# Macaron block on one core: the output projection one round earlier, the turn of h2 moved forward

## The reference

```python
x = L0_attn_x                                      # (1, 1024, 256)
x = x + 0.5 * _L0_ffn_ref(_layernorm(x), ...)      # silu(gate) * up, weights rounded to fp8
x = x + _L0_attn_ref(_layernorm(x), ...)           # retention, below
x = x + 0.5 * _L0_ffn_ref(_layernorm(x), ...)      # the same weights again
...
q, k, v = split(x @ w_qkv);  q, k = _xpos(q), _xpos(k)           # 16 heads of 16
scores = einsum('bhtd,bhsd->bhts', q, k) * D ** -0.5 * mask      # causal, decaying
yn = group_norm(einsum('bhts,bhsd->bhtd', scores, v)) * gn_weight + gn_bias
return (silu(x @ w_g) * yn) @ w_proj
```

## Time and profile before

| what | value |
|---|---|
| time, median of 3 runs | 155.21 us (155.19 to 155.21) |
| the profiled execution's own time | 155.3 us, of which 153.5 us are its span |
| TensorE busy | 147.2 us, 96% of the span |
| VectorE, ScalarE, GpSimd busy | 121.4, 85.2 and 68.5 us |
| TensorE's granted clock | full speed in all slices of the span |

### The profile page before, as it was taken

How to read it: one execution, slowest core, us unless ns; L and a number is a source line. 1 busy time by engine, 2 the same in 40 slices (tenths; PEclk the granted TensorE clock), 3 DMA queues, 4 the chain that set the end, 5 groups by cost and what they waited for, 6 DMA issues and landing times.

```text
span 153.5 us, 3712 instructions
## 1 busy us (share of the span) xinstructions
PE 147.2 (96%) x1327; PEld 117.4 (76%) x1327; DVE 121.4 (79%) x271; ACT 85.2 (56%) x203; POOL 68.5 (45%) x76
## 2 busy tenths in 40 slices
PE   5999899999999999998999999999999999999992
PEld 2366588788989696967686969698877788888991
DVE  0797999999799485859688888899755999566784
ACT  2385998677232453547475656657676648453310
POOL 3447244775891700283845748573978220000000
PEclk9999999999999999999999999999999999999999
DMA  4999502903000000000000000000000000002114
GB/s 112 339 354 306 214 0 31 361 27 121 15 0 0 4 0 4 0 4 0 4 2 0 6 0 6 0 4 0 4 2 0 0 4 0 0 0 68 34 36 139
DMA packets 7009, 8.47 MB, mean 55 GB/s; under 512 B 448, under 2 KB 5712, under 8 KB 6992
## 3 DMA queue, kind: packets, MB, share of 16 engines
q1 hardware_dynamic: 6816, 8.16, 16.0%
q10 hardware_dynamic: 176, 0.07, 0.4%
HBM read 7.19 MB, written 1.05 MB: 54 GB/s over the span
## 4 chain that ended last, share of the span: by engine, by line
PE 74%; POOL 10%; DVE 6%; issue 4%; ACT 3%; DMA 2%; POOLq 0%; ACTq 0%; DVEq 0%
PE bank L1167 23%; PE bank L1195 14%; PE bank L1223 9%; POOL grstd L340 6%; PE bank L1280 5%; PE bank L1236 5%; PE bank L1250 4%; PE bank L1364 3%; PE bank L1309 3%; DMA xt<-in_L_attn_x 2%; POOL rstd L318 2%; PE bank L1262 2%; DVE stats L705 2%; PE bank L1296 1%; PE bank L1341 1%
## 5 line engine op out<-in xcount | busy, mean ns | idle before, releaser
L1167 PE MATMUL bank<-hh,up_r 128*128 128x512 f32 x92 | 25.5, 401 | 0.1
L1167 PE MATMUL bank<-hh,gate_r 128*128 128x512 f32 x92 | 25.6, 401 | 0.0
L1195 PE MATMUL bank<-down_r,fhi 128*128 128x256 f32 x96 | 24.3, 291 | 0.0
L340 POOL TENSOR_TENSOR grstd<-gve,neg_half 128x16 f32<-128x16 f32 x8 | 23.3, 2908 | 0.7
L1195 PE MATMUL bank<-down_r,flo 128*128 128x256 f32 x96 | 23.4, 281 | 0.0
L455 ACT ACTIVATE gact<-bank,vec 128x512 f32<-128x512 f32 x24 | 16.3, 684 | 9.0 <-PE bank L1167 8.1
L463 ACT ACTIVATE fhi<-fuse 128x512 fp32r<-128x512 f32 x24 | 14.6, 624 | 10.8 <-DVE fuse L752 10.8
L1167 PEld LDWEIGHTS bank<-hh,up_r 128*128 128x128 f32 x92 | 16.8, 188 | 4.3 <-issue 0.6
L1167 PEld LDWEIGHTS bank<-hh,gate_r 128*128 128x128 f32 x92 | 16.9, 188 | 4.0 <-ACT gate_r L404 0.4
L1195 PEld LDWEIGHTS bank<-down_r,fhi 128*128 128x128 f32 x96 | 18.1, 188 | 0.7 <-issue 0.2
L1195 PEld LDWEIGHTS bank<-down_r,flo 128*128 128x128 f32 x96 | 18.1, 188 | 0.6 <-issue 0.2
(11 more groups left out here) (90 smaller groups left out, 285.6 us busy)
## 6 DMA issues: line engine op xcount, KB each, us to landing
raw<-in_rotation SPq DMA_DIRECT2D x1, 1536.0 KB, 7.5
out<-xt SPq DMA_DIRECT2D x8, 128.0 KB, 1.8
raw<-in_L_ffn_down_w SPq DMA_DIRECT2D x2, 384.0 KB, 7.4
wqkv<-in_L_attn_w_qkv SPq DMA_DIRECT2D x1, 768.0 KB, 9.3
xt<-in_L_attn_x SPq DMA_DIRECT2D x2, 256.0 KB, 3.7
xt<-in_L_attn_x SPq DMA_DIRECT2D x1, 512.0 KB, 5.4
raw<-in_rotation SPq DMA_DIRECT2D x1, 512.0 KB, 3.5
raw<-in_L_ffn_gate_w SPq DMA_DIRECT2D x1, 384.0 KB, 6.2
```

The lines of the kernel that those rows point to most:

```text
L340: pool.tensor_tensor(grstd[:, c % 2], gve[:, :], neg_half[:, :], ALU.pow).then_inc(grstd_done, 1)
L1167: mm = pe.matmul(dst[:, :], wr[m][:, k * I + i * P:k * I + (i + 1) * P], half[:, k, g % NG, :], start=(k == 0 and half is hhi), stop=(k == ...
L1195: mm = pe.matmul(downs[d][:, 0:C], half[:, g % NG, i, t * P:(t + 1) * P], wr["down"][:, i * C:(i + 1) * C], start=(i == 0 and half is fhi) ...
```

## The change

`project_out` of tile c - 2 now stands in round c, behind `update_state(c)` and ahead of `values(c)`; before, round c held that of tile c - 3, behind `project_g`. `turn_h2(c + 2)` stands directly behind `project_v(c + 1)`, and ScalarE's `copy_h2(c + 2)` ahead of `copy_v(c + 1)`. VectorE's `add_proj(c - 2)` closes the round. Behind the loop `project_out(3)` falls away; VectorE's list for tiles 5, 6 and 7 is set anew, and GpSimd's `group_roots(5)` stands ahead of `add_state(6)`. Two waits in `turn_y` and `project_out` follow the new order.

```diff
--- before.py
+++ after.py
@@ -386,8 +386,8 @@
             add_state(5)
             roots(X_ROOTS + 8)
             roots(X_ROOTS + 9)
+            group_roots(5)
             add_state(6)
-            group_roots(5)
             group_roots(NT - 2)
             group_roots(NT - 1)
             roots(X_ROOTS + NT + 2)
@@ -610,9 +610,9 @@
             copy_y(1)
             for c in range(2, 6):
                 take_y(c - 1)
+                copy_h2(c + 2)
                 copy_v(c + 1)
                 gate_silu(c + 1)
-                copy_h2(c + 2)
                 affine(c - 2)
                 copy_qk(c + 1)
                 copy_y(c)
@@ -976,8 +976,6 @@
                 rotate(c + 1)
                 group_norm(c - 2)
                 mask_scores(c, 2)
-                if c >= 3:
-                    add_proj(c - 3)
                 mask_scores(c, 3)
                 group_var(c - 1)
                 norm_stats(NT + c + 3, NT + c + 4)
@@ -985,12 +983,12 @@
                 rotate_parts(c + 2)
                 mask_kv(c)
                 norm_tile(NT + c + 3)
+                add_proj(c - 2)
             mask_scores(5, 0)
             mask_scores(5, 1)
             rotate(6)
             group_norm(3)
             mask_scores(5, 2)
-            add_proj(2)
             mask_scores(5, 3)
             group_var(4)
             tile_stats(16)
@@ -998,26 +996,26 @@
             mean_var(16)
             gated(3)
             rotate_parts(7)
+            mask_kv(5)
             mean_var(17)
             tile_stats(18)
-            mask_kv(5)
             mean_var(18)
+            add_proj(3)
+            tile_stats(19)
+            mean_var(19)
             mask_scores(6, 0)
             mask_scores(6, 1)
             rotate(7)
             group_norm(4)
             mask_scores(6, 2)
+            mask_scores(6, 3)
             group_var(5)
-            add_proj(3)
-            mask_scores(6, 3)
-            tile_stats(19)
             norm_tile(16)
-            mean_var(19)
+            norm_tile(17)
             mask_kv(6)
-            norm_tile(17)
             norm_tile(18)
+            norm_tile(19)
             gated(4)
-            norm_tile(19)
 
             c, j0 = NT - 1, NG * NI
             mask_scores(c, 0)
@@ -1025,8 +1023,8 @@
             mask_scores(c, 2)
             mask_scores(c, 3)
             add_proj(c - 3)
+            group_var(c - 1)
             group_norm(c - 2)
-            group_var(c - 1)
             tile_stats(2 * NT + 4)
             mean_var(2 * NT + 4)
             gated(c - 2)
@@ -1335,8 +1333,7 @@
                     pe.wait_ge(gd_done, c)
                     if c >= 2:
                         pe.wait_ge(ga_done, c - 1)
-                    if c >= 3:
-                        pe.wait_ge(x2_done, c - 2)
+                        pe.wait_ge(x2_done, c - 1)
                 for k in range(KC):
                     mm = pe.transpose(b_turned_y[c][:, k * P:(k + 1) * P], yT[:, c % 2, k, :], ident)
                 mm.then_inc(y_turned, 1)
@@ -1358,7 +1355,7 @@
                 pe.wait_ge(go_done, c + 1)
                 if c == 0:
                     pe.wait_ge(wp_in, 16)
-                pe.wait_ge(gd_done, min(c + 3, NT - 2))
+                pe.wait_ge(gd_done, min(c + 2, NT - 2))
                 pe.wait_ge(ga_done, c + 1)
                 for k in range(KC):
                     mm = pe.matmul(b_gn[c][:, C:2 * C], go[:, k, :], wp[:, k, :], start=(k == 0), stop=(k == KC - 1))
@@ -1444,21 +1441,19 @@
             for c in range(2, 6):
                 turn_y(c - 1)
                 project_v(c + 1)
+                turn_h2(c + 2)
                 project_g(c + 1)
-                if c >= 3:
-                    project_out(c - 3)
-                turn_h2(c + 2)
                 turn_qk(c + 1)
                 turn_gn(c - 2)
                 project_qk(c + 2)
                 apply_state(c)
                 update_state(c)
+                project_out(c - 2)
                 values(c)
                 scores(c + 1)
             turn_y(5)
             project_v(7)
             project_g(7)
-            project_out(3)
             turn_qk(7)
             apply_state(6)
             update_state(6)
```

## The result

The changed kernel takes 156.55 us (156.37 to 156.96) against 155.19 (155.06 to 155.21): a ratio of 1.0093, with an interval of 1.0079 to 1.0107, 1.36 us slower. The forecast was 156.3, slower, in a range of 155.4 to 157.0. The profiled execution's span is 154.7 us instead of 153.5.

A forecast was written before the change was run, and what follows sets the result against it. TensorE, busy in nearly every slice, was taken to bound the kernel. Costs of +1.88 us in the loop and -0.11, -0.25 and -0.42 behind it gave +1.10, from 155.21 to 156.3, range 155.4 to 157.0.

The forecast's parts named there:

- The place of the projection: Projection between update_state and values, rounds 2 to 5: two changes of array shape cost 0.32 us per round.
- rival (B): Projection between the narrow steps costs nothing beyond its own 0.87 us, so 155.0, no measurable change; chance 0.13.
- (3): Later copy_v, the gated tile and add_proj in the loop are hidden: cost nothing, else TensorE would wait at the projection.
- The wait at `turn_h2`: turn_h2 behind project_v waits for the second mask: 0.23 us in round 2, 0.12 in each of rounds 3 to 5.
- Rival (D): turn_h2 waits for nothing, its signal comes in time: 0.23 and three times 0.12 less, 155.7 us; chance 0.07.
- The loop's sum: Rounds 2 to 5 lengthen by 0.79, 0.34, 0.37 and 0.38: the loop ends 1.88 us later.
- The uncovered wait behind the loop: Without the 0.87 us projection, apply_state(6) behind the loop still waits for gate_silu(7): only 0.11 comes back.
- The two waits for the group norm: Behind the loop, waits of 0.25 us at turn_gn(5) and 0.42 at turn_gn(7) go, as tile 5's root starts earlier.
- Rival (C): Group norm waits behind the loop stay, another wait replacing GpSimd's: the 0.67 gain fails, 157.0 us; chance 0.12.
- The sum: Whole kernel: +1.88 us in the loop, -0.11, -0.25 and -0.42 behind it, +1.10 in all, median 156.3.

The follow-up runs named there:

- e1: Changed kernel with project_out(c - 2) one step earlier, ahead of update_state(c) instead of behind it: 155.35 us, ratio 1.001.
- e2: Changed kernel with turn_h2 between the two halves of project_g, 0.44 us later: 155.68 us, ratio 1.0036.
- e11: As e8, with gate_silu(7) between the halves of copy_v(7) on ScalarE and add_state(6) ahead of group_roots(5) on GpSimd: 153.81 us, ratio 0.9906.
- e3: Changed kernel with GpSimd's order of before, add_state(6) ahead of group_roots(5): 156.57 us, ratio 1.0095.
- e9: Changed kernel with GpSimd's and VectorE's order of before: add_state(6) ahead of group_roots(5), group_norm(5) ahead of group_var(6): 156.46 us, ratio 1.0085.
- e10: As e9, with the statistics of tile 19 late again, tile_stats(19) behind norm_tile(17) and mean_var(19) behind mask_kv(6): 157.14 us, ratio 1.0127.
- e8: Changed kernel with e1, e2 and e4 in one, and ScalarE's gate_silu and affine ahead of copy_v: 153.96 us, ratio 0.9932.
- e4: Changed kernel with turn_gn(4) ahead of apply_state(6) instead of between update_state(6) and values(6): 156.12 us, ratio 1.0062.

## Why the prediction was right, step by step

**The place of the projection** was sized at 0.32 and is 0.30 per round: 0.26 and 1.06, less the plain 0.15 and 0.87. e1 shows that it is the place and not a wait, and that rival (B), the place costing nothing, was wrong. TensorE had `project_qk` and `apply_state` ahead, and the gaps were there. The prediction saw no row that tells whether TensorE loads weights ahead across a change of shape. The weight loads (PEld) of the kernel before do tell; this is the one for the turn of the earlier trace rows:

```profile
105.44 0.20 PEld L1354 LDWEIGHTS bank<-msk,gn 128*128 128x128 f32 x2
```

It begins with the turn itself, while that of the projection of the earlier trace rows, between steps of its own shape, begins at 87.02, 0.10 ahead of its product. Nor was the gated tile late, as (3) had it: in e1 the projection stands 0.36 earlier and waits for nothing.

**The wait at `turn_h2`** was there, but larger: 0.12 was forecast, and `turn_h2` begins 1.31 into round 4 where `project_v` would have released it at 1.14, and loses 0.02 more itself, 0.19. The masks end 1.16 into the round, as forecast, and the turn begins 0.15 behind them: the 0.1 for the signal was too small by 0.05, and the turn's 0.02 was not counted. Four times 0.07, 0.28, is most of what the forecast fell short of. Rival (D), no wait, was wrong; e2 took the wait out and gained 0.87.

**The loop's sum** was 1.88 and is 2.08, by the rounds: 0.85, 0.38, 0.42 and 0.43.

**The uncovered wait behind the loop** came as forecast: `apply_state(6)` stands 3.23 behind the loop's end, to the hundredth. That it waits for `gate_silu(7)` is shown by e11, where that step ends at 103.80 and the wait is gone. What I had not counted is that `apply_state(6)` then takes 0.62 itself instead of 0.53.

**The two waits for the group norm** went, 0.24 and 0.41 for the forecast 0.25 and 0.42. Rival (C), that another wait takes their place, did not come. But the cause I gave is only half right. I named GpSimd's order as what would free tile 5's root. e3 shows the swap to be idle, e9 the one on VectorE too, and e10 shows what did it: the statistics of tile 19, which the earlier projection of tile 3 let come earlier. The prediction had named these statistics as part of the queue, and then credited the wrong part: the size came out right because the same change moved them too.

**The sum.** From the start of round 2 to `turn_gn(7)` the profiled execution needs 51.58 (69.02 to 120.60) instead of 50.12 (69.15 to 119.27), 1.46 more; 1.10 was forecast. The difference is the 0.20 in the loop, the 0.09 of `apply_state`, and 0.08 at `turn_gn(5)`, which passes into the next step in 0.27 where it took 0.19, less some hundredths. The change's gains were real, some 1.5 us: 0.63 in round 2, 0.07 at `turn_gn` in each of rounds 3 to 5, and 0.65 behind the loop. Its costs were some 2.8 us: 1.20 for the place, 0.87 for the masks, and 0.76 in which TensorE stands ahead of `apply_state(6)` (from 105.72, where the four turns' 0.44 are over, to 106.48), where the projection used to run. A part of a version that is faster than both was in it: e8 keeps its order of tiles and changes four places.

## What to carry to other kernels

On an engine that is busy throughout, read the cost of a moved step from its neighbours, start to start: a step of another array shape between two narrow ones costs more than its own length, and moving it by one position can give that back. A wait that is not shown by a bracket shows in the start of the step that waits. Before crediting a reordered queue with a gain, put the old order back: here two reorderings were idle, and what mattered was a result that came earlier.

## What the runs showed of the hardware

A change of the array's shape costs TensorE time on both sides of a short step, also with 2.26 us of long steps directly ahead (`project_qk` at 89.29 to `update_state` at 91.55): 0.30 us for a projection between two steps of 32 columns (0.11 ahead of it, 0.19 behind it), in four rounds, 0.27 for a turn there, behind the loop, and nothing of either once the step stands beside one of its own shape (e1, e4). The Trainium skill (TensorEngine Tiling (Array Packing), Key Properties) says that a change of mode drains TensorE; the runs are in line with that and put these numbers beside it, though they do not show the drain itself.

The same Trainium skill (TensorE: Matmul & The Clock Gate, on the array as sixteen 32x32 parts) says that weight loads are pulled ahead of running products. The rows of the weight loads (PEld) show that between steps of one shape, and not across a change. Round 4 of the changed kernel, with the load for `turn_h2` first:

```profile
87.47 0.20 PEld L1209 LDWEIGHTS bank<-msk,h 128*128 128x128 f32 x2 [0.37 <-issue]
...
91.81 0.73 PEld L1361 LDWEIGHTS bank<-wp,go 128*128 128x128 f32 x4
92.87 0.71 PEld L1307 LDWEIGHTS bank<-sc,v 128*32 128x32 f32 x32 [0.33 <-issue]
```

The load of the projection in e1:

```profile
90.71 0.73 PEld L1361 LDWEIGHTS bank<-wp,go 128*128 128x128 f32 x4
```

In the changed kernel the loads of the projection and of `values` begin with their own products, at 91.81 and 92.87. In e1, behind `apply_state`, the load begins 0.11 ahead of the product at 90.82.

And the bracket of a wait can be missing: TensorE stood 0.17 for the masks in each of rounds 3 to 5, at 87.50 for instance, and no row of its products says so. The row of `project_v`, from 86.47 and 1.03 long, reaches to 87.50 and covers it. In round 2, where that row ends 0.11 ahead of the turn, there is no bracket either. The weight load of the turn, above, has one of 0.37, put down to no engine; in e2 it has none.
